# A decoder layer on one core: the maxima of the following heads run four key tiles ahead instead of five

## What is computed

```python
# self attention
attn = jnp.einsum('bhqd,bhkd->bhqk', q, k) * SCALE
diff = jnp.where(diff > 0, 0.0, diff)                 # key position minus query position
attn = attn + diff * slopes * MAX_BIAS
w = jax.nn.softmax(attn, axis=-1)
out = jnp.einsum('bhqk,bhkd->bhqd', w, v)
# cross attention
attn = jax.nn.softmax(scores, axis=-1)                # 2048 queries, 1601 keys
out = jnp.einsum('bhqk,bhkd->bhqd', attn, v)
# the layer
x = _layernorm(x + attention(x))
x = _layernorm(x + cross_attention(x, ctx))
x = _layernorm(x + experts(x))                        # top 2 of 8 experts
```

## Time and profile before

| what | us |
| --- | --- |
| median of 3 runs | 1904.31 |
| lowest and highest | 1903.47 and 1906.08 |
| the profiled execution | 1906.57 |
| its span in the trace | 1904.8 |
| PE, DVE, ACT busy in the span | 1745.0, 1390.0, 1174.9 |
| first scores of self attention, and of its heads 1, 2, 15 | 157.15, 206.94, 251.12, 825.60 |
| first scores of cross attention, and of its heads 1, 2, 15 | 969.14, 1005.83, 1040.46, 1491.63 |

### The profile page before, as it was taken

One profiled execution on the slowest core, in us unless ns is written; L12 is line 12 of the kernel. 1 busy time (PEld: TensorE's weight loads), 2 busy tenths in 40 slices (PEclk: granted clock), 3 DMA queues, 4 the chain that ended last, 5 costly groups with the idle time before them and its releaser, 6 DMA issues.

```text
span 1904.8 us, 30266 instructions
## 1 busy us (share of the span) xinstructions
PE 1745.0 (92%) x10422; PEld 906.8 (48%) x10422; DVE 1390.0 (73%) x2786; ACT 1174.9 (62%) x2401; POOL 355.5 (19%) x577
## 2 busy tenths in 40 slices
PE   6989999999999999988799999999999877999993
PEld 3433333333333333325444444444444266999993
DVE  7587999999999999914699999999999053010113
ACT  1214777777777777785148777777787842333333
POOL 8120222242222222111000000000000003333331
PEclk9986999999999999999879999999999977999997
DMA  7232000000100000011203001001012126777773
GB/s 261 104 130 73 28 28 28 28 27 32 35 31 31 31 31 28 2 42 63 92 1 101 33 24 39 29 27 40 24 34 78 45 94 188 193 209 194 205 186 105
DMA packets 72880, 141.78 MB, mean 74 GB/s; under 512 B 14156, under 2 KB 47325, under 8 KB 70509
## 3 DMA queue, kind: packets, MB, share of 16 engines
q1 hardware_dynamic: 65018, 129.48, 20.6%
q0 software_dynamic: 7712, 10.37, 3.4%
HBM read 110.71 MB, written 28.45 MB: 73 GB/s over the span
## 4 chain that ended last, share of the span: by engine, by line
PE 73%; DVE 11%; ACT 7%; issue 4%; DMA 3%; SPq 1%; POOL 0%; POOLq 0%; ACTq 0%; DVEq 0%
PE banks L995 21%; PE banks L982 21%; PE banks L940 8%; PE banks L1187 7%; PE banks L1197 7%; ACT XT L1257 5%; PE banks L886 4%; DVE skip L1444 2%; ACT late L1257 2%; DVE wset L1444 2%; DVE CM L1440 2%; DMA oper<-qD 2%; PE banks L951 1%; PE banks L894 1%; DVE banks L1472 1%
## 5 line engine op out<-in xcount | busy, mean ns | idle before, releaser
L1257 ACT ACTIVATE XT<-banks 128x512 f32<-128x512 f32 x1240 | 658.3, 603 | 229.5 <-PE banks L982 160.4
L940 PE MATMUL banks<-oper 52*128 52x512 f32 (+1 forms) x2048 | 712.4, 441 | 32.0 <-DVE CM L1444 12.6
L982 PE MATMUL banks<-oper 54*128 54x512 f32 x1856 | 673.3, 451 | 28.6 <-POOL oper L755 10.5
L982 PEld LDWEIGHTS banks<-oper 54*128 54x128 f32 x1856 | 302.6, 186 | 514.0 <-ACT XT L1257 305.5
L1435 DVE TENSOR_REDUCE CM<-banks 128x1 f32<-128x402 f32 x1024 | 512.8, 566 | 21.1 <-PE banks L940 9.3
L940 PEld LDWEIGHTS banks<-oper 52*128 52x128 f32 x2048 | 347.8, 191 | 139.5 <-DVE CM L1444 63.6
L1257 ACT ACTIVATE late<-banks 128x512 f32<-128x512 f32 x616 | 328.3, 604 | 85.7 <-PE banks L982 71.3
L995 PE MATMUL banks<-XT,VS 128*32 128x512 f32 x2480 | 334.4, 611 | 6.8 <-ACT XT L1257 6.1
L1615 DVE TENSOR_TENSOR YB<-banks,b2E 128x256 f32<-128x256 f32 x39 | 16.5, 424 | 250.0 <-PE banks L1197 250.0
L1336 ACT ACTIVATE HID<-banks,b1E 128x128 f32<-128x128 f32 x312 | 85.1, 381 | 181.3 <-DMA b1E<-in_b1T_dram 169.4
L995 PE MATMUL banks<-late,VS 128*32 128x512 f32 x1232 | 164.9, 607 | 2.9 <-ACT late L1257 2.6
(11 more groups left out here) (205 smaller groups left out, 1393.8 us busy)
## 6 DMA issues: line engine op xcount, KB each, us to landing
W<-in_w1T_dram SPq DMA_DIRECT2D x39, 1024.0 KB
oper<-kD SPq DMA_DIRECT2D x32, 256.0 KB
W2R<-in_w2T_dram SPq DMA_DIRECT2D x8, 1024.0 KB, 7.9
oper<-kxD SPq DMA_DIRECT2D x32, 208.0 KB
b2E<-in_b_dram SPq DMA_DIRECT2D x39, 128.0 KB
qD<-parts SPq DMA_DIRECT2D x8, 512.0 KB, 2.7
kD<-parts SPq DMA_DIRECT2D x8, 512.0 KB, 2.7
oper<-kD SPq DMA_DIRECT2D x32, 128.0 KB
```

What stands on the lines that cost most here:

```text
L940: mm = pe.matmul(slot[:, n * QB:n * QB + ch], QO[64 * g:64 * g + M_ROWS, c2, col:col + P], KO[64 * g:64 * g + M_ROWS, c2, k0:k0 + ch], sta ...
L982: pe.matmul(bank, KO[64 * g:64 * g + S_ROWS, c, b * P:(b + 1) * P], QO[64 * g:64 * g + S_ROWS, c, q0:q0 + QB], start=True, stop=True).then ...
L1257: act.activation(PT[(c * plan.nu + u) % PRING], score_bank(plan, u, h, c), ACT.Exp).then_inc(A.exps, 1)
```

## The change

`LEAD` becomes 4. Block b carries the slot b + 4, in self attention and in cross attention.

```diff
 HALF = N // 2
 SUM_AT = 2
-LEAD = 5
+LEAD = 4
 WIDE = 4 * (SUM_AT + 1)
```

## The result

| what | before | after |
| --- | --- | --- |
| median of 20 runs each, us | 1905.49 | 1900.46 |
| lowest and highest | 1900.12, 1913.94 | 1897.22, 1927.98 |
| the profiled execution | 1906.57 | 1897.30 |
| its span | 1904.8 | 1895.5 |

The account below looks back on a forecast made before the run. The prediction took the loop through the scores' three banks, 2.61 us a block, as the bound, with DVE just under it. Terms -2.70 - 2.43 - 0.13 + 4.34 = -0.92 took 1904.31 to 1903.4 us, range 1898.6 to 1906.2.

Parts of the forecast that it names:

- The prologues: Before the first scores: self loses two maxima of ten, -2.70 us; cross loses five of 24, -2.43 us.
- Head 14: Self head 14: the shift comes after key tile 12's cast, which then waits for nothing, -0.13 us.
- The shift's DMAs: They start one block, 2.6 us, later in each head; 3.2 us are left before the next head, so 0.
- The shift and the cast: Self heads 0 to 13: shift moves off key tile 12's cast, two gaps follow one another, 0.31 us each, +4.34.
- DVE's two idle stretches: Sign in self heads 1 to 13: two near key tiles 12 and 13, 0.3 to 0.6 each, replacing one of 0.58.
- Cross heads: All slots rotate by one block, with no cast: 0, bound 0.1 us a head; heads unchanged at 34.63.
- the trade of block kinds: Blocks with two table reduces or one are exchanged: 0, bound 0.1 us either way a head.
- The first: Rival, self heads: the shift carries its stall along, nothing is added, only prologues count; 1899.0 us, chance 0.22.
- The second: Rival, self heads: key tile 12's late cast costs its full 0.64 us a head anew; 1908.0 us, chance 0.07.
- The third: Rival, both heads 0: the clock rises at the same moment, losing 1.2 us of the gain; 1904.6, chance 0.11.
- The fourth: Rival, self prologue: no shorter, since first scores wait for something else at 154.5; 1906.1 us, chance 0.03.
- The chances: For the whole kernel's time: faster, below 1900.5, 0.24; slower, above 1908.1, 0.06; no difference 0.70.

Follow-up runs that it names:

- e1: The changed kernel again, lead of four in both attentions, timed against the kernel before: 1901.50 us, ratio 0.9993.
- e8: The changed kernel a third time, lead of four in both attentions, against the kernel before: 1900.12 us, ratio 0.998.
- e10: Lead of five kept, only key tile 12's cast called for earlier in self heads, against the kernel before: 1901.85 us, ratio 0.9988.
- e9: Lead of four in both attentions, only key tile 12's cast called for earlier in self heads, against the kernel before: 1898.89 us, ratio 0.9964.
- e5: The kernel before, lead of five, timed again against itself: 1904.92 us, ratio 1.0013.
- e12: Lead of three in cross attention alone, five in self attention, against the kernel before: 1900.18 us, ratio 0.9971.
- e7: Lead of three in both attentions, against the kernel before: 1914.80 us, ratio 1.006.
- e11: Lead of three in self attention alone, five in cross attention, against the kernel before: 1917.10 us, ratio 1.0059.
- e3: Lead of four in cross attention alone, five in self attention, against the kernel before: 1904.62 us, ratio 0.9994.

## Why the prediction was right, and where it was off

**The prologues.** Right in mechanism. Self: -2.70 forecast; the first scores fell at 154.74, near the 154.5 named. That match is partly luck, since e1 and e8, the same code, have 157.07 and 157.47 with a shift that itself came 2.8 us later; the distance from the shift is what counts. Shift to first scores is 16.7 us as the mean of six traces with a lead of five (16.16 to 17.58) and 13.7 of six with four (13.42 to 13.88): -3.0, which the spread doesn't tell from -2.70. Cross: -2.43 forecast, -2.82 in every pair of traces. The reduces' price of 0.486 held. What was missed is 0.39 us in front of S0, which starts 0.49 after the prologue's last maximum before and 0.10 after it now. I had counted only the prologue's own items, and not that `LEAD` also changes which query block S0 takes.

**Head 14.** -0.13 forecast, -0.08 measured for heads 14 and 15 together.

**The shift's DMAs.** 0 forecast, 3.2 us left; measured 0 and 3.3. With a lead of three 0.73 are left, still without a wait.

**The shift and the cast.** The layout of head 2 gave the values at 282.80, 285.77, 289.14 and 292.00. Put on the same start (4.61 us are added, since head 2 begins at 246.51 instead of 251.12), they were at 282.82, 285.80, 289.15 and 291.92. The distances named beforehand were 2.97, 3.37 and 2.86; they are 2.98, 3.35 and 2.77. The step that was off is the last: I let the first reduce of block 13 start 0.92 after the maximum's matmul, as in the block of the shift before, and it started 0.81 after (283.43 to 284.24). Its values followed 3.07 later, exactly as laid out. So the term is +0.23 a head and not +0.31, or 14 x 0.23 = +3.2 instead of +4.34. DVE's two idle stretches were foreseen as 0.3 to 0.6 each and measured 0.23 and 0.47, the first below what was named.

The missing 0.11 can be seen in S0. Before, the cast of key tile 12 on POOL and the S0 that waits for it, behind the maximum at 285.09:

```profile
284.87 0.29 POOL L755 CAST oper<-zeros 4x128 fp32r<-4x128 f32 x1 [5.11 <-PE banks L982]
...
285.30 0.47 PE L982 MATMUL banks<-oper 54*128 54x512 f32 x1
```

and after, the S0 behind the maximum at 283.43:

```profile
283.53 0.47 PE L982 MATMUL banks<-oper 54*128 54x512 f32 x1
```

Before, S0 starts 0.21 after the maximum and 0.14 after the cast's end at 285.16. Where the cast isn't late, it starts 0.10 after the maximum: in after, and in e10 (280.14 behind 280.04). So the distance of 0.92 that the layout borrowed from the old place held 0.11 us of the cast's own lateness, the very thing that was to be taken apart.

The Trainium skill, Perfetto Trace Analysis, Identifying Performance Opportunities, says that a gap repeating on the engine that should be saturated can mean that there isn't enough SBUF or PSUM for the next tile. The runs agree in part for the shift's own gap: it moved with the two-slot ring at no cost (44.15 and 44.16), but no run gave the ring a third slot. They show also what the rule doesn't say, that a second wait had been lying in that gap and got a price when the gap moved away.

**The rest.** Cross heads 34.62 against 34.63; the trade of block kinds left nothing that can be seen.

**The sum by measured steps** is -3.0 - 2.8 - 0.1 + 3.2 = -2.7, against -0.92 forecast. So 1.1 us of the error is the head's term, 0.4 the start of cross attention, and 0.3 the self prologue, which is within its spread. The pooled comparison gives -3.1 (1.9 to 4.2), and the steps are enough for it. That the first comparison still fell into the range is partly luck: of its -5.0 us the steps account for 2.7, and the other 2.3 are near the 1.8 by which two medians of the same code differ.

**The rivals.** The first, nothing added to the heads, would have given -5.3 and stands refuted by every trace, though the first comparison alone (-5.0 us) looks just like it. Who goes by the median alone would take it for the cause. The second, 0.64 a head, doesn't hold at this lead; at three the cast's own distances give it (0.65). The third, that the clock's rise stays where it is, isn't borne out at this lead. In cross attention the rise came 8.5 to 8.6 us after the first scores in five of six traces with a lead of four (13.3 in e9), and 8.3 to 12.6 us after them in six with five. In self attention it came 8.6 to 12.8 us after them with four, and 6.9 to 20.2 with five. From the cross shift's transpose on, five of six rises with four came after 17.1 to 17.2 us (21.9 in e9), those with five after 19.7 to 24.1. So it moved along. The two stretches of after, which answer to the earlier trace rows:

```profile
154.74:167.50 12.76, 12.76 (x47) 0.50 0.62 146
961.19:969.64 8.45, 8.45 (x34) 0.50 0.00 0
```

It varies from run to run of one kernel; before (49.79 us for head 0) and e5 (45.47) are the same code. The Trainium skill, TensorE: Matmul & The Clock Gate, Part 1, says so too, but with half a us either way; here, in two traces of the same code, it rose 20.2 and 8.6 us after the first self scores. At a lead of three the third rival may have its place: e12's 17.06 us, against 12.54 in e7 with the same cross lead, which is too little to tell. The fourth, a prologue that gets no shorter, is refuted.

**The chances.** A gain of 0.2% or more had 0.24, mostly on a rival that is wrong. The first comparison says 0.28% faster, all runs together 0.16%, which lies just inside of no difference.

## What to carry to other kernels

A wait that costs nothing may be lying under another one. Before moving a stall, lay out the program around its old place and its new one, and price each neighbouring late event there by the nearest place where it stands alone. The one distance that was taken from a place where two waits meet is the one that was off. Here that gave four start times within 0.1 us, and the better edit as well: ordering the blocks so that the casts come early gives 11 us where moving the lead gives 3.

When an edit is worth a fifth of a per cent, read it step by step in several traces: one kernel against itself differed by 1.8 us in the median.

## What the runs showed of the hardware

The spread of run times goes with the clock. Over the runs of one kernel the time rises by 1.1 to 1.6 us for each 0.001 by which the mean granted clock falls: e11's fastest run is 1903.54 us at 0.963, its slowest 1939.9 at 0.938. The stretches of half clock also lie in head 15, where nothing but scores, exponentials and values runs. There 30.7 us of half clock cost 10.85 us, 0.35 per us; in cross heads 14 and 15 of e3 17.07 us cost 6.5, 0.38 per us. And one change of the order seems to push a kernel into them: with a self lead of three 20 of 24 runs are as long as if they held such a stretch, though only the two traces of e7 and e11 show it directly.
